# Constant matmuls ahead of three group sums in a shift-and-convolve, group-norm and Hadamard kernel

## What is computed

```python
x = x + displace(group_norm(x), offset)   # 48 offsets, 8 channels each
x = x + hadamard(group_norm(x))           # 384 channels padded to 512, times H/sqrt(512)
```

## Time and profile before

| what | us |
|---|---|
| median of 3 runs | 261.75 |
| lowest, highest run | 259.67, 261.84 |
| the profiled execution's own time | 261.49 |
| its span from first to last instruction | 259.5 |
| PE busy in it | 143.3 |
| VectorE busy in it | 197.5 |
| ScalarE busy in it | 136.2 |

### The profile page before, as it was taken

One profiled execution on the slowest core, in us unless ns is written; L12 is line 12 of the kernel. 1 busy time (PEld: TensorE's weight loads), 2 busy tenths in 40 slices (PEclk: granted clock), 3 DMA queues, 4 the chain that ended last, 5 costly groups with the idle time before them and its releaser, 6 DMA issues.

```text
span 259.5 us, 2305 instructions
## 1 busy us (share of the span) xinstructions
PE 143.3 (55%) x616; PEld 87.5 (34%) x616; DVE 197.5 (76%) x321; ACT 136.2 (52%) x217; POOL 44.7 (17%) x49
## 2 busy tenths in 40 slices
PE   0000000508507249867920696999999999988610
PEld 0000000408507249756920532443333333333200
DVE  0799999999972169845760336999999999999940
ACT  1000999779761046035500199997788878880000
POOL 0000000000000053211233784000404184000000
PEclk9999999955955558997985559999999999999975
DMA  5999999999999208999960567219999999998798
GB/s 158 420 408 411 407 411 285 370 412 406 412 283 244 65 2 237 248 301 315 283 154 18 145 216 250 99 81 327 356 334 417 399 419 368 390 405 348 285 407 341
DMA packets 24845, 76.78 MB, mean 296 GB/s; under 512 B 6576, under 2 KB 6832, under 8 KB 24544
## 3 DMA queue, kind: packets, MB, share of 16 engines
q1 hardware_dynamic: 18928, 67.07, 71.7%
q0 software_dynamic: 5072, 9.51, 11.6%
q10 hardware_dynamic: 832, 0.05, 0.2%
HBM read 67.07 MB, written 29.99 MB: 374 GB/s over the span
## 4 chain that ended last, share of the span: by engine, by line
DVE 38%; DMA 33%; PE 9%; ACT 5%; issue 5%; SPq 5%; POOLq 0%; DVEq 0%
DMA ring<-x_pad 27%; DVE ring L934 22%; DVE parts L271 10%; PE ps L573 4%; PE ps L554 4%; DMA blk<-x_pad 4%; ACT blk L518 3%; DVE blk L271 2%; ACT parts L526 2%; DMA stat_rows<-blk_stat 2%; PE ps L563 2%; SPq L301 1%; SPq L289 1%; DVE halfstat L799 1%; DMA stat<-stat_rows 1%
## 5 line engine op out<-in xcount | busy, mean ns | idle before, releaser
L934 DVE SCALAR_TENSOR_TENSOR ring<-ps,beta,ring 128x1024 f32<-128x1024 f32 x48 | 59.8, 1280 | 0.0
L635 PE MATMUL ps<-parts,had_sb 128*128 128x512 f16 x216 | 54.0, 384 | 8.1 <-DVE parts L271 5.8
L563 PE MATMUL ps<-geo_sb,blk 128*128 128x128 f32 x72 | 12.5, 336 | 59.0 <-DMA blk<-x_pad 45.4
L799 DVE BATCH_NORM_STATS2 halfstat<-ring 128x6 f32<-128x512 f32 x64 | 38.9, 674 | 1.8 <-DMA ring<-x_pad 1.8
L573 PE MATMUL ps<-parts 128*128 128x160 f32 (+2 forms) x180 | 33.0, 348 | 10.4 <-ACT parts L460 10.4
L283 POOL DMA_INDIRECT ring<-x_rows,row_at x24 | 30.2, 1257 | 46.3 <-DMA ring<-x_pad 39.9
L518 ACT ACTIVATE blk<-ring,gn 128x1024 f32<-128x1024 f32 x32 | 37.8, 1226 | 0.0
L271 DVE TENSOR_TENSOR parts<-blk,parts 128x1024 f16<-128x1024 f32 x27 | 32.9, 1219 | 6.0 <-ACT parts L526 6.0
L573 PEld LDWEIGHTS ps<-parts 128*128 128x128 f32 x180 | 31.5, 225 | 11.4 <-ACT parts L460 10.6
L635 PEld LDWEIGHTS ps<-parts,had_sb 128*128 128x128 f16 x216 | 20.1, 99 | 44.0 <-DVE parts L271 13.2
L645 PE MATMUL ps<-ring,first_w 128*128 128x512 f32 x64 | 32.0, 624 | 0.0
(11 more groups left out here) (117 smaller groups left out, 136.6 us busy)
## 6 DMA issues: line engine op xcount, KB each, us to landing
ring<-x_pad SPq DMA_DIRECT2D x20, 1536.0 KB, 15.3
out<-ring SPq DMA_DIRECT2D x13, 1536.0 KB, 7.4
blk<-x_pad SPq DMA_DIRECT2D x15, 512.0 KB, 17.2
out<-ring SPq DMA_DIRECT2D x9, 512.0 KB, 6.0
x_rows<-blk POOLq DMA_DIRECT2D x6, 512.0 KB, 6.6
other_a<-x_pad SPq DMA_DIRECT2D x2, 512.0 KB, 9.1
x_rows<-other_a POOLq DMA_DIRECT2D x2, 512.0 KB, 6.5
geo_sb<-geo SPq DMA_DIRECT2D x1, 683.0 KB, 4.7
```

What stands on the lines that cost most here:

```text
L563: last = pe.transpose(pixels[:, j // 4, 128 * (j % 4):128 * (j % 4 + 1)], shifted[:, 128 * j:128 * (j + 1)], eye)
L635: last = pe.matmul(ps[n % 4][:, h, :], had_sb[:, sign, :], part_of(n, t, part)[:, 512 * h:512 * (h + 1)], start=False, stop=ends and part ...
L799: last = dve.bn_stats(halfstat[:, i % 4, t, h, :], ring[:, t, place_of(i), 512 * h:512 * (h + 1)])
L934: dve.scalar_tensor_tensor(ring[:, m, place_of(i), :], ps[n % 4][:, :, :].rearrange("p a n -> p (a n)"), beta[:, i % BATCH:i % BATCH + 1], ...
```

## The change

A helper `turn_over(count)` is added to PE's program. It issues `count` matmuls of constants: the 128x128 identity (`eye`) as weights and 512 columns of the group matrices as the moving side, in float32, into bank 1 of `ps[1]`, each starting anew. Nothing reads the result, and no wait or signal goes with it. It is called with 12 between `convolve(1)` and `group_sums(1)`, with 6 between `group_sums(2)` and the wait for `gn_done`, and with 9 (`TURNS`) after the branch for further offsets, ahead of `group_sums(3)`. Nothing else changes.

```diff
+TURNS = 9
...
+            def turn_over(count):
+
+                for _ in range(count):
+                    pe.matmul(ps[1][:, 1, :], eye, geo_sb[:, G_SUM:G_SUM + 512], start=True, stop=True)
+
             pe.wait_ge(conv_w_done, 1)
             for k in range(EARLY):
                 transposes(k)
             for k in range(EARLY):
                 convolve(k)
+            turn_over(12)
             group_sums(1, 0, lambda b: stat[:, b, :, 0])
             group_sums(2, 1, lambda b: moment[:, b, 1, :])
+            turn_over(6)
             pe.wait_ge(gn_done, 1)
             transposes(EARLY)
...
+            turn_over(TURNS)
             group_sums(3, 0, lambda b: moment[:, b, :, :].rearrange("p k b -> p (k b)"))
```

## The result

| | before | changed |
|---|---|---|
| median of 20 runs each, us | 262.56 | 260.3 |
| lowest and highest, us | 259.67, 264.96 | 256.98, 261.37 |
| profiled execution, us | 261.49 | 260.56 |
| its span, us | 259.5 | 258.6 |

The ratio is 0.990 with a 95% interval of 0.9874 to 0.9925. On 262 us that is 2.6 us faster, between 2.0 and 3.3. This ratio and the later ones leave out executions more than 1.5% above the fastest of their kernel; the medians in the table are of all runs and lie 2.3 us apart. The forecast was 4.2 us and 257.3. The sign was right; the median lies 0.1 us above the range, and the gain is about six tenths of the forecast.

A forecast was written before the change was run, and what follows sets the result against it. The prediction took a chain of transfers and serial PE, ACT and DVE work to bound the kernel, with PE at half clock where it stands on it. 261.49 - (2.1 + 0.9 + 1.2) = 257.3 us, range 255.2 to 260.2.

The forecast's parts named there:

- The constants and their price: Constant matmuls on PE: 0.86 us each at full clock; twelve need 10.3 us, ending about when the first sums could start.
- Second sums: Second group sums, behind the first: partly at full clock, gain 1.1 us, bounds 0 and 1.5.
- What the write meets: Group values' write, issued 2.5 us earlier, meets draining block loads; 2.1 us of gain remain, bounds 1.5 and 2.5.
- the first sums' 1.4 us: First group sums at full clock behind the twelve: gain 1.5 us less 0.1 of overrun.
- Transposes: PE's transposes of block 2, behind the six: mostly at full clock, gain 0.9 us, bounds 0 and 0.9.
- rival 2: Clock lost too soon: second sums, transposes or third sums run at half; gain only 2.0, 259.5 us; chance 0.17.
- Blocks: Block stage, its transfers at 0.97: the 3.0 us gained ahead of it carry through; faster PE work alone gives nothing there.
- The late cold stretch: Low clock in the blocks at about 120 us: 1.7 us of slow convolution on the chain, left in.
- rival 1: The low clock in the blocks at 120 us also goes: 255.6 us; chance 0.12.
- Third sums: Third group sums, behind the nine: partly at full clock, gain 1.2 us, bounds 0 and 1.5.
- Rival 3: The blocks swallow the early gain and only the third sums' 1.2 us remain: 260.3 us; chance 0.05.
- Rival 4: Constants don't hold the clock, the twelve end 6.3 us late: slower, 269.7 us; chance 0.06.

The follow-up runs named there:

- only 12: The changed kernel without the 6 and the 9 constant matmuls; ratio to the kernel before 0.9958, 1.1 us faster.
- only 9: The changed kernel without the 12 and the 6 constant matmuls; ratio to the kernel before 0.9988, 0.3 us faster, not told from no change.
- 12 and 6: The changed kernel without the 9 constant matmuls ahead of the third sums; ratio to the kernel before 0.9916, 2.2 us faster.
- one between: The changed kernel plus one constant matmul between the first and second group sums; ratio to the kernel before 0.9892, 2.8 us faster.
- four in blocks: The changed kernel plus four constant matmuls after the convolution of block 5; ratio to the kernel before 0.9888.
- eleven: The changed kernel with 11 in place of 9 constant matmuls ahead of the third sums; ratio to the kernel before 0.9905.
- load later: The changed kernel with the third plain block load issued right behind the write of the group values; ratio to the kernel before 0.9922.
- all three: The changed kernel plus four constant matmuls after block 5's convolution, 11 in place of 9, third plain load behind the write; ratio to before 0.9917.
- eighteen: The changed kernel with 18 in place of 12 constant matmuls ahead of the first sums; ratio to the kernel before 1.0067.
- all places: The changed kernel plus one constant matmul between the sums, four after block 5's convolution, 11 for 9; ratio to before 0.9848, 4.0 us faster.
- short second sums: The changed kernel with three of seven matmuls in the second group sums, so the variance is incomplete; ratio to the kernel before 0.9897.

## Why the prediction was right or wrong

The traces, each with its numbers read from the timelines and the records of single packets: how long the three sums took; the issue of the `gn_rows` write, the end of the last packet of the block loads, the landing of the write, and the start of DVE's mask of block 2 (L836 in the kernel before), all four counted from the start of DVE's last image moments; and the time from that mask to DVE's last block moments.

| kernel | sums 1, 2, 3 | issue | loads' end | landing | mask | mask to last moments |
|---|---|---|---|---|---|---|
| before | 3.17, 3.17, 3.20 | 12.2 | 11.7 | 13.9 | 21.4 | 37.7 |
| changed | 1.84, 3.17, 2.11 | 10.9 | 11.8 | 12.6 | 19.2 | 41.0 |
| changed, again | 1.74, 2.46, 1.81 | 10.1 | 11.9 | 12.7 | 19.3 | 36.0 |
| only 12 | 1.74, 2.18, 3.20 | 9.8 | 12.3 | 13.1 | 20.6 | 38.7 |
| only 9 | 3.17, 3.17, 2.95 | 12.2 | 11.1 | 13.9 | 21.4 | 38.5 |
| 12 and 6 | 1.74, 3.17, 3.20 | 10.8 | 11.9 | 12.8 | 19.5 | 37.9 |
| one between | 1.74, 3.17, 1.75 | 10.8 | 12.1 | 13.1 | 19.7 | 38.0 |
| four in blocks | 1.74, 1.93, 3.08 | 9.5 | 11.9 | 12.7 | 20.2 | 37.5 |
| eleven | 1.74, 3.17, 1.75 | 10.8 | 12.1 | 13.2 | 19.8 | 39.3 |
| load later | 1.74, 3.17, 1.75 | 10.8 | 14.7 | 12.5 | 20.6 | 39.6 |
| all three | 1.89, 3.17, 1.75 | 10.9 | 14.6 | 12.6 | 20.7 | 37.5 |
| eighteen | 1.63, 1.73, 1.75 | 13.9 | 12.0 | 15.6 | 22.2 | 39.1 |
| all places | 1.74, 3.17, 2.06 | 10.8 | 12.0 | 13.0 | 19.7 | 38.3 |
| short second sums | 1.63, 0.84, 2.46 | 8.5 | 12.0 | 12.9 | 20.4 | 39.6 |

**The constants and their price: right.** 12 take 10.46 us and 18 take 15.61, so 0.86 for each more; they hold the clock; and they fit ahead of the sums. In the ten traces with twelve (the short second sums not among them) the first sums take 1.74 us eight times, and 1.84 and 1.89, against 1.70 forecast.

**Second sums: wrong in size, and without effect.** The term was 1.1 us. In the ten traces with twelve they average 2.88 us, a gain of 0.3, and in seven of the ten they gain nothing, because the clock falls before they start. The forecast let the twelve end at 78.7, with the sums; that hung on the end of the convolutions in one execution. In these seven the twelve ended 0.5 to 1.2 us ahead of the sums. In the three others they ended within 0.2 us of the sums' start, and the second sums had the full clock for a part, as in the second trace of the changed kernel (timeline of PE):

```profile
67.78 10.46 PE L603 MATMUL ps<-geo_sb 128*128 128x512 f32 x24
78.43 1.74 PE L555 MATMUL ps<-stat,geo_sb 128*128 128x16 f32 x14 [0.18 <-DVE scrap L832]
81.19 2.46 PE L555 MATMUL ps<-moment,geo_sb 128*128 128x16 f32 x14 [1.03 <-DVE moment L829]
```

Where they took 2.46, 2.18 and 1.93 us, the write landed after 12.7, 13.1 and 12.7 us, no earlier than in the others.

**What the write meets: this is the step that failed.** The mechanism was named and is real; the size was off. The forecast took the loads' end as 86.3 and let the write land 0.4 us later, at 86.7, which is 11.8 after the last image moments began, and so kept 2.1 us. With twelve and the loads unmoved, the landings lie at 12.6 to 13.2 whether the write was issued 10.9 us (changed) or 8.5 us (short second sums) after them. The gain that remains is 13.9 less 12.9 on average, 1.0 us and not 2.1. The forecast's lower bound of 1.5 was too high as well. It read 86.3 from a share averaged over 16 engines; by the packet records of the same trace the last load packet ended at 86.55, and in the nine traces with twelve and unmoved loads it ended 11.8 to 12.3 us after the last image moments began, not 11.4. From there to the landing it is 0.7 to 1.1 us, not 0.4. In the short second sums the write's first packets passed at 84.4, a microsecond after its issue, and its last at 87.2, behind the last load packet at 86.9: most of the write was through, and the landing waited for the rest. Every saving on the chain beyond the first sums' 1.4 us is lost here, and a part of these 1.4 too. That the second sums gained 0.3 in place of 1.1 did not matter, since where they were fastest the landing was no earlier. The changed kernel's landing at 85.25 + 1.7 = 86.95 us looks like the forecast's 86.7, but that is luck: in this execution the last image moments began 0.5 us earlier than in the one before.

**Transposes: near.** With the six, the mask starts at 19.2 to 20.2, on average 19.6, and 1.8 us earlier than before (the two kernels with the moved load left out, whose fetches are later). Less 1.0 from the landing, the transposes give 0.8; the term was 0.9. From landing to mask it is 7.5 us where the transposes of block 2 run at half clock and 6.6 or 6.7 where they run at full. With the six they were at half in two traces, four in blocks and short second sums, in which the clock fell at 93.1 and 93.3, just ahead of them or as they began: the loss that rival 2 feared. The six never ran into the transposes: in the changed kernel they ended 0.25 us ahead, having run half cold as the forecast allowed.

**Blocks: right that the shift carries, and a warning on single traces.** Eighteen made the kernel 4.2 us slower, twelve and six 2.2 us faster. From mask to last moments the traces need 36.0 to 41.0 us, and the two of the same changed kernel are the two ends. That spread of 5 us is larger than the whole forecast gain, and the two executions' own times, 260.56 and 255.85 us, differ by nearly as much; the 3.5 us that the changed kernel's first trace lost at one block transfer were part of it.

**The late cold stretch: right to leave it in, its price too high.** The clock fell between 109 and 121 us in every trace in which no constants stood there, so rival 1 did not come about. Its 1.7 us stood on the chain, yet removing 2.1 us of slow PE work gained 0.3, with 1.5 as the most that the interval allows.

**Third sums: near in the traces, not shown in the times.** The seven traces with the nine (eighteen and the load later among them, the short second sums not) have 2.17 us on average, a gain of 1.0; the term was 1.2. In the two with 2.95 and 3.08 the clock fell 0.3 and 0.2 us after the sums began, close to the fall in the gap that was given as the risk. Eleven had 1.75. In time the nine alone gained 0.3 us, between -0.4 and 1.0, so the term of 1.2 lies outside what that kernel gained, and the whole change gained 0.4 more than twelve and six, which two chips can't resolve.

**The sum.** 1.0 + 0.8 + 1.0 = 2.8 us, inside the measured 2.0 to 3.3. The times of the parts give much the same, 2.2 + 0.3 = 2.5. The forecast was 2.1 + 0.9 + 1.2. The single largest miss is the landing. Of the 3.0 us between 257.3 and 260.3 these terms are 1.4. Another 1.1 is the base: the forecast was made against an execution of 261.49, and the kernel before had a median of 262.56 in the 20 runs beside the change. The last 0.5 us is not explained and no larger than what such medians leave open.

**Rivals.** Rival 2 (clock lost too soon) holds in part: the second sums were lost in most traces. The measured 260.3 lies in its range of 258.6 to 260.4, but partly because of the base. Rival 3 was refuted. That its 260.3 us is the measured median to the tenth is chance; it stood for a gain of 1.2 us. Its shape, though, was right at another place: it is the transfer ahead of the blocks that swallows, not those in them. Rival 4 was refuted by a clock of 1.00 through the twelve.

## What to carry to other kernels

When a chain piece is shortened ahead of a small transfer, look at what the DMA engines still hold at that moment, and take the end of the slowest engine, not of the average share, as the floor for the landing. Matmuls of constants kept TensorE at full clock here and cost nothing where PE waited anyway. The group sums behind them were not safe: the clock fell 2.6 to 5.3 us after the last constant matmul of the twelve, eighteen, nine or eleven, where the forecast had counted on 2.7 to 4.1 from two falls. So look at the time from the last dense matmul to the end of the work that shall be fast, in more than one trace. Where one stage varies by 5 us from execution to execution, as the blocks did here, compare landmarks ahead of it, over several traces, before a cause is read out of two.

## What the runs showed of the hardware

- The write on ACT's queue was held up as much as that on SP's: in the two traces with SP's issues at 84.2 and 83.4 it took 3.5 and 4.5 us against SP's 3.3 and 4.4. SP's queue held the block loads, ACT's did not. The prediction cited the Trainium skill (DMA: Bandwidth & Descriptors, Queues, rings and completion order) for a queue's descriptors being consumed in ring order on each engine; these rows show that a queue of its own does not avoid the delay, so the order within SP's ring is not needed to explain it. Whether the engines or the memory behind them hold it up was not tried.
- During the group sums before the change the clock stayed at 0.50. In all seven traces with twelve whose second sums took 3.17 us it fell from 1.00 between 79.5 and 81.4 us, from the first sums on to the start of the second. With eighteen it stayed at 1.00 through both sums and fell at 88.2, some 5 us after the last constant matmul.
- One dense matmul of 0.86 us between the sums did not keep the clock from falling at 81.3 and 81.2 in the two kernels that had it.
